# Products of an expert group ahead of the routed tokens, gate activations and residual one group later

## The reference, cut to what matters

```python
# dense experts (4), part of s
hid = silu(einsum('btd,efd->btef', h, w1) + b1)
eo  = einsum('btef,edf->bted', hid, w2) + b2
s   = x + einsum('bte,bted->btd', gw, eo)
# routed experts (16, at most 160 tokens each), y
xe  = x_flat[idx]                                  # gather by expert
out = gelu(xe @ W1 + b1) @ W2 + b2
y   = x_flat.at[safe_idx].set(out, mode='drop')    # back to the tokens
# end of the layer, then the statistics of the next layer norm
x   = x + s * silu(y)
```

## Time and profile before

| | |
|---|---|
| median of 3 runs | 1257.19 us (1256.74 to 1260.31) |
| profiled execution | 1261.83 us |
| its span, from the first to the last instruction | 1259.8 us |
| busy over the span | PE 1171.1 (93%), DVE 802.2 (64%), POOL 812.9 (65%), ACT 674.1 (54%) |
| PE busy in the stretch 388 to 1260, the second layer | 845.26 of 872.00 |
| granted TensorE clock, mean | 0.965 of full speed |

### The profile page before, as it was taken

The page is one execution under the profiler, slowest core; times in us unless marked ns, Lnnn a source line. Parts: engine busy times, 40 slices in busy tenths (PEclk is TensorE's granted clock), DMA queues, the critical chain, the costliest instruction groups (busy, mean ns, idle before and its releaser), DMA issues.

```text
span 1259.8 us, 31159 instructions
## 1 busy us (share of the span) xinstructions
PE 1171.1 (93%) x11813; PEld 760.6 (60%) x11820; DVE 802.2 (64%) x2017; ACT 674.1 (54%) x1375; POOL 812.9 (65%) x1097
## 2 busy tenths in 40 slices
PE   4898679998986999999999999999999999999997
PEld 2354455567753656666665666676666676666665
DVE  3787446741556577668668658757767766865552
ACT  2533152235422466656656656666665665665665
POOL 1777300040404487787887878878778788787886
PEclk9998778999987999999999999999999999999998
DMA  8200200001302332030230221203203013022001
GB/s 320 104 1 1 75 1 1 1 30 46 103 6 59 69 87 44 8 79 10 44 78 18 44 55 41 44 19 77 43 8 80 15 39 81 15 44 60 19 2 35
DMA packets 74752, 60.09 MB, mean 48 GB/s; under 512 B 38950, under 2 KB 69162, under 8 KB 73516
## 3 DMA queue, kind: packets, MB, share of 16 engines
q1 hardware_dynamic: 73580, 56.02, 18.0%
q0 software_dynamic: 1024, 2.09, 0.6%
HBM read 19.70 MB, written 4.72 MB: 19 GB/s over the span
## 4 chain that ended last, share of the span: by engine, by line
PE 61%; ACT 3%; DVE 2%; issue 1%; DMA 1%; DVEq 0%; ACTq 0%
PE S L1737 9%; PE S L1738 9%; PE S L1739 9%; PE A L1727 9%; PE O L1751 5%; PE O L1752 5%; PE O L1749 5%; PE M L1718 2%; PE M L1695 2%; PE M L1697 2%; PE M L1696 2%; ACT prob L1947 1%; ACT otok L1961 1%; PE M L1712 1%; DMA shifted<-turned 1%
## 5 line engine op out<-in xcount | busy, mean ns | idle before, releaser
L1479 POOL TENSOR_TENSOR plow<-prob 128x512 f16<-128x512 f32 (+3 forms) x640 | 576.9, 915 | 110.3 <-ACT prob L1947 88.1
L1947 ACT ACTIVATE prob<-S,keep_sigma 128x512 f32<-128x512 f32 (+3 forms) x640 | 385.0, 626 | 269.7 <-PE S L1739 269.2
L2049 DVE CUSTOM_DVE_ANT_0 junk<-A,mask_rows,part 128x512 bf16<-128x512 f32 (+3 forms) x384 | 249.7, 650 | 105.2 <-PE A L1727 67.9
L1749 PE MATMUL O<-V,prob 128*128 128x65 f16 x2176 | 232.6, 193 | 0.2 <-POOL plow L1479 0.2
L1751 PE MATMUL O<-V,prob 128*128 128x64 f16 x2176 | 232.4, 194 | 0.0
L1752 PE MATMUL O<-V,plow 128*128 128x65 f16 x2176 | 231.6, 192 | 0.0
L1737 PE MATMUL S<-rows 97*128 97x512 f16 (+3 forms) x640 | 222.9, 348 | 5.8 <-ACT prob L1947 4.3
L1738 PE MATMUL S<-rows 96*128 96x512 f16 (+3 forms) x640 | 222.3, 347 | 0.0
L1739 PE MATMUL S<-rows 96*128 96x512 f16 (+3 forms) x640 | 219.0, 345 | 0.0
L1749 PEld LDWEIGHTS O<-V,prob 128*128 128x128 bf16 x2176 | 203.3, 97 | 21.2 <-POOL plow L1479 0.3
L1751 PEld LDWEIGHTS O<-V,prob 128*128 128x128 bf16 x2176 | 202.2, 97 | 19.3
(11 more groups left out here) (352 smaller groups left out, 1869.4 us busy)
## 6 DMA issues: line engine op xcount, KB each, us to landing
rows<-stage_rows SPq DMA_DIRECT2D x64, 256.0 KB, 3.4
V<-stage_v SPq DMA_DIRECT2D x16, 516.0 KB, 4.6
W<-in_W SPq DMA_DIRECT2D x2, 2048.0 KB
shifted<-turned SPq DMA_DIRECT2D x32, 128.0 KB, 2.3
rows<-stage_pos SPq DMA_DIRECT2D x64, 64.0 KB, 3.1
w<-in_w SPq DMA_DIRECT2D x2, 1024.0 KB
xe_rows<-zero SPq DMA_DIRECT2D x1, 1280.0 KB, 9.2
ye_rows<-xe SPq DMA_DIRECT2D x5, 256.0 KB, 3.0
```

Of the source, the lines that this page charges most:

```text
L1479: pool.tensor_tensor(plow[:, k % PB, 0:w], full, full.bitcast(BF16).rearrange("p (q e) -> p q e", e=2)[:, :, 1], ALU.subtract).then_inc(s_ ...
L1749: pe.matmul(both, high[:, cs, 1], vh[h][:, j, 0:HS + 1], start=(j == 0 and s == 0), stop=False, skip_group_check=True)
L1947: act.activation(prob[:, k % PB, 0:w], S[k % 2][:, 0:w], ACT.Exp, scale=sigma[:, 2 * p + h:2 * p + h + 1]).then_inc(s_exp, 1)
L2049: dve.tensor_tensor_reduce(junk[:, g % 2, 0:w], A[g % 2][:, 0:w], add, -1.0, before, ALU.add, ALU.min, out).then_inc(s_max, 1)
```

## The change

PE: at n = 10 second(10) stands ahead of `routed()` instead of behind it. DVE: at n = 10 add(10), which reads what second(10) made, likewise. ACT: the four gate activations, with the wait for the last gather ahead of them, move from n = 12 to n = 13, that is from behind the hidden activations of group 13 to behind those of group 14. DVE: x1 and statistics1 of the chunks 0 and 1, which stood behind add(12) and add(13), now both stand behind add(13). No operation is added, removed or changed in size, and no transfer is issued at another place of its queue.

```diff
@@ PE @@
                 if n + 1 < len(GROUPS):
                     first(n + 1)
                 if n == ROUTED_AT:
+                    second(n)
                     routed()
                 weights1(n)
-                second(n)
+                if n != ROUTED_AT:
+                    second(n)
@@ ACT @@
-                elif n == ROUTED_AT + 2:
+                elif n == ROUTED_AT + 3:
                     act.wait_ge(s_ga, 16 * NT)
                     for c in range(NC):
                         act.activation(g[:, tiles(c), :], y_tok[:, tiles(c), :], ACT.Silu).then_inc(s_sg, 1)
@@ DVE @@
                 if n == ROUTED_AT:
+                    add(n)
                     routed()
...
-                add(n)
-                if n in (ROUTED_AT + 2, ROUTED_AT + 3):
-                    x1(n - ROUTED_AT - 2)
-                    statistics1(n - ROUTED_AT - 2)
+                if n != ROUTED_AT:
+                    add(n)
+                if n == ROUTED_AT + 3:
+                    for c in range(2):
+                        x1(c)
+                        statistics1(c)
```

## The result

The changed kernel takes 1248.89 us, the median of 4 runs (1246.60 to 1252.04), against 1257.95 for the kernel before on the same chip (4 runs): the ratio is 0.9915, interval 0.9891 to 0.9939. It is faster by 9.1 us, where 12.3 were forecast; the forecast for the median was 1244.9 in a range of 1241 to 1250. Two more comparisons of the same two kernels, made with the experiments, gave 10.7 us (1249.77 against 1260.44) and 12.3 us (1247.32 against 1259.63). The interval of the first ratio alone is 7.7 to 13.7 us, so the medians can't tell these gains from each other or from the forecast; what follows goes by the rows.

A forecast was written before the change was run, and what follows sets the result against it. PE was taken to bound the kernel (61% of the chain of waits), through three holes and low clock behind the long ones. Savings 3.57 + 0.40 + 0.9 + 7.42 = 12.29 us from 1257.19 gave 1244.9 us, range 1241 to 1250.

The forecast's parts named there:

- (a): PE's hole before the transposes: second(10) moved into it saves 3.57 us, bounds 0 and 3.57.
- (c): Transposes of the gathered tokens: with the hole shrunk the clock does not fall, saving 0.9 us, bounds 0 and 1.8.
- R1: Rival: the clock falls at the transposes all the same, so their 0.9 us gain goes; 1245.8 us, chance 0.22.
- (b): First(12): ACT's SiLU table load starts earlier, so PE's 0.40 us hole goes; bounds 0 and 0.40.
- (d): First(14) to second(13): gates behind group 14 save 7.42 us, 4.50 hole and 2.92 clock; bounds 0 and 7.42.
- R2: Rival: the gather's wait comes back at group 15, with a hole of 3.1 us; 1250.9 us, chance 0.10.
- R4: Rival of other sign: gates before group 15 cost more than before group 14; 1258 with gathers 12 us later, chance 0.03.
- (e): Block's end: DVE's later chain costs nothing, 2.2 us spare; POOL's weight preparation, if it sticks out, under 1 us.
- (f): Second(14) and second(15): low clock behind one-column products stays, 9.48 us against 7.14; may vary up to 3.6 either way.
- R3: Rival: the routed start's hole was hidden anyway or second(10) pushes the routed part; 1246.7 with half, chance 0.08.

The follow-up runs named there:

- products_only: Kernel before with only second(10) and add(10) moved ahead of the routed part; 1257.01 us against 1260.44, ratio 0.9977, chip A.
- before_again: Kernel before, unchanged, run for its trace on chip C, where engines stand still; 1269.49 us, one run.
- gates_only: Kernel before with only the gates, x1 and statistics1 moved; 1252.08 us against 1260.44, ratio 0.9932, chip A.
- changed_third: The changed kernel once more, against the kernel before, on chip A; 1247.32 us against 1259.63, ratio 0.9900.
- changed_again: The changed kernel once more, in the same rounds as its two halves, chip A; 1249.77 us against 1260.44, ratio 0.9913.
- scales_first: Changed kernel with DVE's scales() directly behind group 14's column maxima; 1248.56 us against the kernel before's 1260.44, ratio 0.9908, chip A.
- scales_second: Changed kernel with DVE's scales() between x1(2) and statistics1(2); 1262.86 us against the kernel before's 1266.91, ratio 0.9983, chip B.
- columns_spread: scales_second with line 972's one-column products strewn through second(14); 1264.59 us against the kernel before's 1266.91, ratio 0.9992, chip B.
- hole_filled: Kernel before plus 20 unread 128x128 products between first(14)'s second and third product; 1271.72 us against 1266.91, ratio 1.0058, chip B.

## Why the prediction came out as it did

The forecast median, 1244.9, was 4.0 us below the measured 1248.89, which lies in the range. The sum was 12.29; the stage gave 11.74. By its steps:

- (a) and (c), second(10) in the first hole and the clock at the transposes: 3.57 + 0.9 = 4.47 forecast. Measured 0.22 on the way to the transposes and 4.41 from there to first(12), 4.63 (in products_only 0.38 + 4.41 = 4.79). If 3.57 of the 4.41 are (a), then 0.84 are (c); before_again, whose order was not changed, has 0.74 for the same place without the hole. The hole that was left was 0.35, forecast 0.5 to 0.7. R1, that the clock falls all the same, is refuted by 1.00 in 292 to 300.
- (b), the table load: 0.40 forecast, 0.48 measured (22.35 to 21.87). By the drain that the Trainium skill, ScalarE: Activation LUTs, section What ACT_TABLE_LOAD costs, puts behind a load it would have been nothing. The measurement decides against it: the load began at 320.66 and the next activation at 322.94, 2.28 us later and after a wait for PE, where load and drain would be 2.66.
- (d), the gates: 7.42 forecast and 7.42 measured in the changed kernel, 7.43 in gates_only. First(15) has no hole, which refutes R2 and R4 on chip A. The margin was mis-sized, to the good side: the gates ran from 350.00 to 352.19, where 349.7 to 351.9, moved by the 1.82 of the late start, would be 351.5 to 353.7. Counted from first(11) the gathers ended 2.43 us earlier than before (62.19 against 64.62), not 0.9; products_only has 62.00 and changed_third 62.25. Where the other 1.5 us come from is open. ACT then waited 3.33 us for PE, where I had 1.9.
- (e) is the step that failed: "So (e) costs nothing with 2.2 us to spare", with "if it sticks out, by under 1 us" for POOL. The maxima came at 361.22; the forecast 359.3, moved by the 1.82 of the late start, is 361.1. So the chain of DVE was placed rightly. What I missed is that POOL's part of the block must end 3.15 us before the second layer, DVE's only 0.54. I had compared POOL with add(15) and found a lead of 3.3, and took no price for the meeting itself. The block's last part grew by 0.79 (26.54 to 27.33), where the sum has 0. That is a loss of 2.42 from add(15) to the second layer (3.32 to 5.74), less 1.63 by which PE came sooner to add(15), because the low stretch of (f) was smaller in this execution. This second part was luck; had PE been as quick before, 25.51 as in before_again and products_only, the last part would have grown by 1.82 and the stage given 10.7. In changed_third, whose low stretch is like that of before in size, 0.81 of it sticks out (4.13 - 3.32 from add(15) to the second layer), so the aside held. Where PE is quick it is more, the 2.42 of the first trace.
- (f), the low stretch, moved as I had allowed, 8.93 to 10.08 us for second(14) and second(15) over three executions of the changed kernel. But it moves nothing there, as POOL covers it: the last part is 27.33 to 27.35 in all three. Its two-sided term belonged to the kernel before alone.

The terms that I took from rows, (a) to (d), sum to 12.53 measured, less 0.79 is 11.74. The 2.7 us between the 9.1 of the medians and 11.7 aren't in the stage; the medians scatter (9.1, 10.7, 12.3), and the late start of 1.82 is an example of why. My range had put this scatter down to the low stretch of (f), so that it held the result for another reason than the one I gave. Part of the scatter lies ahead of the stage: in 160 to 200 us the granted clock is 0.68 in the first trace of the changed kernel, which came to first(11) at 287.81, and 0.79 and 0.78 in products_only and changed_third, which came at 282.48 and 283.28. It isn't all: changed_again had 0.76 there and came at 286.84, and its second layer was 2.8 us shorter. R3, as a matter of one execution or another, found nothing on chip A: in all its traces the tokens landed after PE was there. On B and C something like it is the rule, for a reason that R3 didn't have.

On DVE beside POOL: 1.77 and 1.76 us for 12 elements, 1.97 for 0.69, and nothing of the sort where POOL's operation is cut or gone. The Trainium skill, SBUF — State Buffer, section SBUF: two separate sides, says that DVE and GpSimd share a pair of ports as an exclusive lock that the first holds for its whole instruction, and that of DVE's instructions those with two SBUF inputs or in a two-port mode take part. These traces agree: the multiplications that were held, in scales_first and in the changed kernel, have two SBUF inputs, and the adds, which read PSUM, took 1.12 us beside POOL in changed_third. Which mode the held TENSOR_SCALAR of scales_second ran in, no run here shows. In the changed kernel it cost nothing, since POOL's end, 3.15 ahead, covered it. That the low clock comes with the hole is borne out by all traces of chip A (hole gone, clock 1.00; hole 7.14, clock 0.50). The experiment made for it had no hole, but before_again shows it apart from the order of the work, in one execution on another chip. No run filled a hole that was there with other work and changed nothing else.

## What to carry to other kernels

An engine that waits for a transfer is best given work that has long been ready, and the wait itself put in a queue behind as much as its followers can spare: here two moves took 11.7 us out of the stage, 3.8 of them clock behind the holes. A saving upstream of a transfer's wait is given back in part at that wait (here 2.6 of 5.3 us), so move both. Where engines meet at the end of a block, each has a price of its own there; read from the rows how long before the meeting each must be done, before counting its lead as cover.

## What the runs showed of the hardware

- A block's end costs 3.15 us behind POOL's last instruction or 0.54 behind DVE's, whichever is later, in all 14 traces.
- A DVE operation of 12 elements was held for 1.76 us by a POOL operation of 1.89; the adds that read PSUM kept their 1.12 to 1.13.
- The granted clock was 0.50 for some 13 us (376 to 389, one execution of columns_spread) with PE busy in every record, while one-column products stood among 128x128 ones.
- In the trace of the kernel before, the last two products of first(14), behind a hole of 4.50 us, took 3.78 us, those of first(12), behind one of 0.40, 1.98.
- The same kernel takes 1258 to 1260 us on one chip and 1267 to 1269 on two others, where ACT stood still for up to 9.3 us (hole_filled), and PE with it, beside POOL's indirect transfers, with no instruction named that it waited for. On the first chip POOL issued the same transfers and nothing stood still.
